# Gather indices copied by GpSimd itself, in halves of four, in a graph kernel on one Trainium2 core

## The chip, the cores and the metric

The kernel runs on one core of one Trainium2 chip. The metric is the device time of one execution in microseconds (us). Three runs of the kernel before gave 2215.43, 2211.89 and 2213.24 us, a median of 2213.24 us.

## The reference

There are 6250 nodes with 64 features each and 200000 edges, sorted by destination. Every edge takes the features of its source node, `xs = x[src]`, and five graph operators sum functions of it over the edges of each destination node:

```python
norm = edge_weights / jnp.sqrt(deg_w[src] * deg_w[dst])
gcn = seg(norm[:, None] * xs) @ Wgcn + bgcn
sage = x @ Wsage_s + seg(xs) / deg_c[:, None] @ Wsage_n + bsage
agg_w = seg(edge_weights[:, None] * xs)
gin = ((1.0 + gin_eps) * x + agg_w) @ Wgin + bgin
gconv = x @ Wgc1 + agg_w @ Wgc2 + bgc
eop = seg(edge_weights[:, None] * jax.nn.relu(xs + edge_attr)) @ Wedge + bedge
```

`seg` is the sum by destination. The five results are mixed with five weights, added to x and normalised along the features.

## The kernel before

The edges are cut into 196 chunks of 1024: 8 tiles (`TILES`) of 128 edges, one edge per partition. A chunk needs the features of its 1024 source nodes and the inverse root of their degree. Chunks get them in three ways. Chunks 0 to 15 (`EARLY`) gather raw x by an indirect DMA in the setup, before degrees are known. Chunks 16 to 35 (`PICKED`) get them by TensorE: one-hot matrices times the node table, which lies in SBUF (L1280, the picks). Chunks 36 to 195, the 160 late chunks (`LATE`), gather rows of the node table from HBM: one indirect DMA per tile, 8 per chunk, all issued by GpSimd (L559). The early chunks' remaining work is woven between the first 16 late chunks, and the picked chunks' work between the next 140 (five rounds of 28 late and 4 picked chunks). So the late chunks' loop is nearly the whole program.

A late chunk passes through the engines like this. GpSimd issues its 8 gathers into slot u of a ring of four (`feat[:, u]`, `UNROLL` = 4). VectorE (L950, L953) waits for `gathered[u]` and adds the edge attributes; ScalarE applies the ReLU (L655); VectorE weighs the one-hot matrices of the destinations (L1076); TensorE multiplies (16 matmuls of L1261) and increments `chunk_product`. GpSimd may fill the slot again only then: it waits for `chunk_product` at L556, four chunks on. Between late chunks TensorE does the picks (14 matmuls of L1280 per tile), ScalarE builds their one-hot matrices (L688, L691) and VectorE reduces them (L988, L992). Every engine works through its own list in order.

The gathers read their row numbers from `idx`, a tile at fixed addresses, [128, 4 slots, 8 tiles]. All row numbers lie in `e_src`, which a transposition in the setup fills: TensorE transposes, ScalarE copies the result out of PSUM (L590) and increments `flip_used`. ScalarE also moves row numbers from `e_src` to `idx`: for the first four late chunks once (L592), and then, at every odd slot, for the pair of slots whose gathers have landed (L650 to L653), 128x16 numbers in one copy, which increments `staged`. GpSimd waits for `staged` (L555) and for `chunk_product` (L556) ahead of each chunk. `e_src` is longer by four chunks than it need be, and L593 fills the rest, so that the last step of ScalarE's copies has something to read.

`gathers_begun` is a semaphore that nobody waits for; its increment at L557 carries the wait. In the setup GpSimd also issues the 128 gathers of the early chunks (L526): those of the first three chunks (`HEAD`) at once, the rest behind the wait for `base_stored` at L542, from the seventh chunk on paced by `weight_done` of VectorE. Then it waits for the node table in HBM (`table_stored`), and the late loop begins.

Of the kernel before, what the change touches and what calls it, by code (L numbers as in the profile page):

```python
# [27 lines left out]
U32 = mybir.dt.uint32  # L28
# [4 lines left out]
P = 128  # L33
N, D = 6250, 64
E = 200000
TILES = 8
CHUNK = P * TILES
CHUNKS = -(-E // CHUNK)
LAST_START = E - CHUNK
LAST_OLD = (CHUNKS - 1) * CHUNK - LAST_START  # L40
UNROLL = 4
# [7 lines left out]
BASE = EARLY + PICKED  # L49
LATE = CHUNKS - BASE  # L50
LATE_STEPS = LATE // UNROLL
# [20 lines left out]
HALF = TILES // 2  # L72
# [13 lines left out]
def build(nc, x, src, dst, edge_attr, edge_weight, mix, Wgcn, bgcn, Wsage_s, Wsage_n, bsage,  # L86
          gin_eps, Wgin, bgin, Wgc1, Wgc2, bgc, Wedge, bedge, out):
    ctx = ExitStack()
    with ctx:
        def sb(name, shape, dt=F32):  # L90
            return ctx.enter_context(nc.sbuf_tensor(name, shape, dt))
# [4 lines left out]
        def sem(name):  # L96
            return ctx.enter_context(nc.semaphore(name))
# [35 lines left out]
        base_row = sb("base_row", [1, CHUNKS], I32)  # L133
        passes = sb("passes", [1, 1], I32)

        e_src = sb("e_src", [P, CHUNKS + UNROLL, TILES], U32)
        e_dst = sb("e_dst", [P, CHUNKS, TILES])
        e_win = sb("e_win", [P, CHUNKS, TILES], BF16)

# [42 lines left out]
        idx = sb("idx", [P, UNROLL, TILES], U32)  # L182
# [101 lines left out]
        gathers_begun, windows_set = sem("gathers_begun"), sem("windows_set")  # L284
# [3 lines left out]
        base_ready, base_flipped, base_stored = sem("base_ready"), sem("base_flipped"), sem("base_stored")  # L288
        rows_ready, flipped, flip_used = sem("rows_ready"), sem("flipped"), sem("flip_used")
        dst_flip_used = sem("dst_flip_used")  # L290
        src_wrapped, w_lifted = sem("src_wrapped"), sem("w_lifted")
        cuts_set, sign_done, weight_done = sem("cuts_set"), sem("sign_done"), sem("weight_done")
        deg_chain, windows_moved = sem("deg_chain"), sem("windows_moved")
        deg_product, deg_added = sem("deg_product"), sem("deg_added")
# [4 lines left out]
        staged = sem("staged")  # L299
        gathered = [sem(f"gathered{u}") for u in range(UNROLL)]  # L300
# [4 lines left out]
        chunk_product = sem("chunk_product")  # L305
# [21 lines left out]
        FLIPS = 3 * 2 * (TILES // 4)  # L327
        DST_FLIPS = FLIPS // 3
# [14 lines left out]
        def node_tiles(k):  # L343

            return range(k * NODE_TILES, min((k + 1) * NODE_TILES, NT))
# [158 lines left out]
        def _(pool):  # L504
# [19 lines left out]
            def gather_early(c):  # L524
                for j in range(TILES):
                    nc.gpsimd.indirect_dma_start(  # L526
                        out=early_x[:, c, j], out_offset=None, in_=x,
                        in_offset=bass.IndirectOffsetOnAxis(ap=early_idx[:, c, j:j + 1], axis=0),
                    ).then_inc(early_gathered, 16)

            for c in range(HEAD):
                gather_early(c)
                if c == 0:
# [5 lines left out]
                    nc.gpsimd.memset(table_sb[:, :, D:TROW], 0.0).then_inc(pad_x, 1)  # L539
                    nc.gpsimd.memset(table_sb[:, N % NT:, 0:D], 0.0).then_inc(pad_x, 1)  # L540

            pool.wait_ge(base_stored, 1)  # L542
            n_pass = pool.value_load(passes[0:1, 0:1], min_val=1, max_val=WINDOWS)
            with pool.Fori(0, n_pass) as v:
                pool.wait_ge(product_g, v * UNITS + 2)
                pool.sem_inc(gathers_begun, 1)
                for c in range(HEAD, EARLY):
                    if c > PACED:
                        pool.wait_ge(weight_done, 2 * (c - PACED) - 1)
                    gather_early(c)  # L550
                pool.wait_ge(table_stored, 16)
                with pool.Fori(0, LATE_STEPS) as i:
                    for u in range(UNROLL):
                        it = v * LATE + i * UNROLL + u
                        pool.wait_ge(staged, v * (LATE // 2) + i * (UNROLL // 2) + u // 2 + 1)  # L555
                        pool.wait_ge(chunk_product, it + 1)  # L556
                        pool.sem_inc(gathers_begun, 1)  # L557
                        for j in range(TILES):
                            nc.gpsimd.indirect_dma_start(  # L559
                                out=feat[:, u, j, D:BLOCK], out_offset=None, in_=table,  # L560
                                in_offset=bass.IndirectOffsetOnAxis(ap=idx[:, u, j:j + 1], axis=0),
                            ).then_inc(gathered[u], 16)

        @block.scalar
        def _(act):
# [23 lines left out]
                        act.wait_ge(flipped, q)  # L589
                        nc.scalar.copy(flip_place(to, g, n, half), flip_of(q, n)).then_inc(flip_used, 1)  # L590
            act.wait_ge(flip_used, FLIPS - DST_FLIPS)
            nc.scalar.copy(idx[:, :, :], e_src[:, BASE:BASE + UNROLL]).then_inc(staged, UNROLL // 2)  # L592
            nc.scalar.copy(e_src[:, CHUNKS:CHUNKS + UNROLL], e_src[:, BASE:BASE + UNROLL]).then_inc(src_wrapped, 1)  # L593
            act.wait_ge(src_wrapped, 1)
            act.wait_ge(base_stored, 1)
            n_pass = act.value_load(passes[0:1, 0:1], min_val=1, max_val=WINDOWS)
            with act.Fori(0, n_pass) as v:
# [34 lines left out]
            for k in range(NODE_GROUPS):  # L632
                tiles = node_tiles(k)
# [12 lines left out]
            with act.Fori(0, n_pass) as v:  # L646
                act.wait_ge(early_gathered, early_landed(v))

                def late_chunk(i, u):
                    if u % 2:  # L650
                        act.wait_ge(gathered[u - 1], (v * LATE_STEPS + i + 1) * (16 * TILES))
                        act.wait_ge(gathered[u], (v * LATE_STEPS + i + 1) * (16 * TILES))
                        nc.scalar.copy(idx[:, u - 1:u + 1], e_src[:, bass.ds((i + 1) * UNROLL + u - 1 + BASE, 2)]).then_inc(staged, 1)  # L653
                    act.wait_ge(summed_in, v * LATE + i * UNROLL + u + 1)
                    nc.scalar.activation(feat[:, u, :, 0:D], attr[:, u], ACT.Relu).then_inc(relu_ready, 1)  # L655

# [70 lines left out]
            for g in range(GROUPS + 1):  # L727
# [5 lines left out]
                if g > 0:  # L733
                    tiles = slice((g - 1) * GROUP, g * GROUP)
# [631 lines left out]
```

## Time and profile before

| what | value |
|---|---|
| three runs | 2211.89 to 2215.43 us, median 2213.24 us |
| the profiled execution | 2228.75 us |
| its span | 2226.9 us |
| TensorE matmul (PE) busy | 1556.4 us, 70% |
| GpSimd (POOL) busy | 1355.2 us, 61% |
| VectorE (DVE) busy | 928.6 us, 42% |
| ScalarE (ACT) busy | 826.9 us, 37% |
| mean granted TensorE clock | 0.867 of full |

The span is the time from the first to the last instruction of the one profiled execution, on which all rows below rest; its own time is 2228.75 us, 15.5 us (0.7%) above the median of the three runs. Busy is the time in which an engine works on an instruction; waiting, branching and semaphores don't count. In an answer of the timeline the columns are the start, the duration, the engine, the source line, the operation, output<-input, and in brackets the idle time of the engine before the row and what ended it: "issue" means nothing that the profile shows, "remote" a semaphore whose setter the profile doesn't find close by. The ends of matmuls are modelled.

### The profile page before, as it was taken

To read this page: it belongs to the slowest core of one execution; us is meant where nothing else is said; L and a number is where in the kernel's file an instruction comes from. 1 tells how busy PE (TensorE), PEld (TensorE's weight loads), DVE (VectorE), ACT (ScalarE), POOL (GpSimd) and SP (SyncE) were. 2 spreads that over 40 slices of the span, in tenths; PEclk is the share of its full clock that TensorE was granted. 3 is DMA by queue.
4 is the path that set the end of the run, shared out by engine and by line. 5 is a ranking of instruction groups with operands and counts; after the bars stand their busy time and mean duration, and the time that the engine had idled before them with its cause. 6 is when DMAs were issued, how large, how long until landed. Compare 5 with 4: busy or idle time off the path is not lost.

```text
span 2226.9 us, 22565 instructions
## 1 busy us (share of the span) xinstructions
PE 1556.4 (70%) x6037; PEld 1007.5 (45%) x6037; DVE 928.6 (42%) x2539; ACT 826.9 (37%) x1201; POOL 1355.2 (61%) x1426
## 2 busy tenths in 40 slices
PE   1004367566888777877878778777887888877876
PEld 1003367553554544544445445444444445544546
DVE  5684256543433332433433433243333334423346
ACT  1676233243433433424244234233333324423323
POOL 7665366556666656656666666566666656665660
PEclk9999967688989888978889888888888888888988
DMA  5111234331222222222222222222222222222223
GB/s 98 23 24 51 70 100 112 95 80 42 51 64 45 55 54 46 57 46 44 54 57 53 47 57 43 47 58 50 48 66 43 48 51 57 47 53 44 59 55 77
DMA packets 83186, 126.12 MB, mean 57 GB/s; under 512 B 29494, under 2 KB 31269, under 8 KB 82821
## 3 DMA queue, kind: packets, MB, share of 16 engines
q0 software_dynamic: 45056, 48.85, 13.6%
q1 hardware_dynamic: 36371, 74.90, 11.0%
q10 hardware_dynamic: 1650, 1.04, 0.2%
q8 instruction: 53, 0.87, 0.2%
q14 instruction: 56, 0.46, 0.1%
HBM read 121.29 MB, written 3.40 MB: 56 GB/s over the span
## 4 chain that ended last, share of the span: by engine, by line
PE 43%; issue 18%; another core or an unknown queue 17%; DVE 10%; ACT 4%; POOL 3%; DVEq 2%; DMA 1%; SPq 0%; POOLq 0%; ACTq 0%
PE psum L1280 27%; PE psum L1261 13%; ACT ring L604 4%; POOL ring L559 3%; DVE ring L1076 2%; DVE sums L1065 2%; DVE early L988 1%; PE psum L1312 1%; PE psum L1228 1%; DVE attr L953 1%; DVE early L992 1%; DMA ring<-node_table,idx 1%; PE psum L1341 1%; PE psum L1342 1%
## 5 line engine op out<-in xcount | busy, mean ns | idle before, releaser
L559 POOL DMA_INDIRECT ring<-node_table,idx x1280 | 1228.4, 960 | 758.2 <-issue 389.4
L1280 PE MATMUL psum<-table_sb,early_x 128*128 128x455 f32 x2240 | 988.1, 586 | 115.6 <-issue 110.1
L1280 PEld LDWEIGHTS psum<-table_sb,early_x 128*128 128x128 f32 x2240 | 446.0, 205 | 573.4 <-issue 566.7
L1261 PE MATMUL psum<-ring 128*128 128x120 f32 x2560 | 405.3, 313 | 246.5 <-issue 127.5
L1261 PEld LDWEIGHTS psum<-ring 128*128 128x128 f32 x2560 | 375.5, 224 | 310.2 <-issue 164.9
L988 DVE TENSOR_TENSOR early<-psum,digit_hot 128x455 f32<-128x455 f32 x160 | 100.6, 631 | 989.5 <-remote 599.3
L688 ACT ACTIVATE early_x<-early,minus_ids 128x256 f32<-128x256 f16 x560 | 370.4, 744 | 138.7 <-remote 103.4
L655 ACT ACTIVATE ring<-attr 128x512 f32<-128x512 f32 x160 | 100.2, 626 | 483.4 <-DVE attr L953 383.8
L679 ACT ACTIVATE early<-early 128x256 f32<-128x256 f32 x40 | 16.7, 416 | 518.2 <-DVE early L1009 385.1
L1065 DVE TENSOR_TENSOR sums<-sums,psum 64x40 f32 (+1 forms) x648 | 127.5, 197 | 97.4 <-remote 53.6
L526 POOL DMA_INDIRECT early_x<-in_x,early_idx x128 | 122.0, 953 | 61.4 <-issue 40.3
L1261 PE MATMUL psum<-early 128*128 128x120 f32 x576 | 102.7, 340 | 77.8 <-issue 53.7
L1076 DVE TENSOR_TENSOR ring<-ring,psum 128x320 f32<-128x320 f32 x320 | 141.6, 484 | 6.0 <-issue 1.0
L691 ACT ACTIVATE early_x<-early_x,ones 128x1792 f32<-128x1792 f32 x80 | 143.1, 1788 | 2.6
L1261 PEld LDWEIGHTS psum<-early 128*128 128x128 f32 x576 | 98.0, 251 | 98.5 <-issue 72.7
L953 DVE TENSOR_TENSOR attr<-attr,ring 128x512 f32<-128x512 f32 x160 | 109.6, 685 | 0.0
L877 DVE SCALAR_TENSOR_TENSOR early<-attr,scratch,psum 128x1024 bf16<-128x1024 f32 x80 | 98.1, 1275 | 24.2 <-issue 22.6
L992 DVE TENSOR_REDUCE early<-early 128x65 f32<-128x455 f32 x160 | 98.5, 627 | 4.2
L1236 PE MATMUL psum<-ring 128*128 128x98 f32 (+1 forms) x8 | 2.0, 435 | 137.8 <-DVE ring L894 137.8
L604 ACT ACTIVATE ring<-attr,scratch 128x1024 bf16<-128x1024 f32 x82 | 93.0, 1137 | 10.6 <-issue 10.4
L1070 DVE TENSOR_TENSOR ring<-e_win,psum 128x320 f32<-128x320 f32 (+1 forms) x160 | 77.1, 482 | 18.2 <-issue 11.4
L1236 PEld LDWEIGHTS psum<-ring 128*128 128x128 f32 (+1 forms) x8 | 1.8, 327 | 138.0 <-DVE ring L894 138.0
(158 smaller groups left out, 644.8 us busy)
## 6 DMA issues: line engine op xcount, KB each, us to landing
attr<-in_edge_attr SPq DMA_DIRECT2D x79, 512.0 KB
ring<-node_table,idx POOLq DMA_INDIRECT x1280
early<-in_edge_attr SPq DMA_DIRECT2D x36, 256.0 KB
src_all<-in_src SPq DMA_DIRECT2D x16, 512.0 KB
early<-key_rows SPq DMA_DIRECT2D x10, 512.0 KB
early_x<-degree_rows SPq DMA_DIRECT2D x2, 1568.0 KB
early_x<-in_x,early_idx POOLq DMA_INDIRECT x128
node_table<-table_sb SPq DMA_DIRECT2D x1, 1666.0 KB, 6.0
```

The lines of the kernel that those rows point to most:

```text
L526: nc.gpsimd.indirect_dma_start(out=early_x[:, c, j], out_offset=None, in_=x, in_offset=bass.IndirectOffsetOnAxis(ap=early_idx[:, c, j:j + ...
L559: nc.gpsimd.indirect_dma_start(out=feat[:, u, j, D:BLOCK], out_offset=None, in_=table, in_offset=bass.IndirectOffsetOnAxis(ap=idx[:, u, j: ...
L604: last = nc.scalar.activation(signs[0:rows, k % TURNS], row_dst[0:rows, g], ACT.Sign, bias=cuts[0:rows, n:n + 1], scale=-1.0, accum_out=si ...
L688: last = nc.scalar.activation(to[:, :, a], keys[:, tile:tile + 2], ACT.Square, bias=minus_ids[:, a:a + 1])
L691: nc.scalar.activation(to, to, ACT.Relu, bias=ones[:, 0:1], scale=-2.0).then_inc(node_hot_made, 1)
L953: nc.vector.tensor_tensor(out=attr[:, u], in0=attr[:, u], in1=feat[:, u, :, D:2 * D], op=ALU.add).then_inc(summed_in, 1)
L988: nc.vector.tensor_tensor(out=picks[:, k % 2], in0=pick_ps[k % 2].rearrange("p (b c) -> p c b", b=SPLIT), in1=hot_c, op=ALU.mult).then_inc ...
L992: last = nc.vector.tensor_reduce(out=feat_g[:, half, k, D:2 * D + 1], in_=picks[:, k % 2], axis=AX.X, op=ALU.add)
L1065: last = nc.vector.tensor_tensor(out=sums[of, k, to], in0=sums[of, k, to], in1=acc[ps, part * WINDOW:(part + 1) * WINDOW], op=ALU.add)
L1076: return nc.vector.tensor_tensor(out=to[:, :, k], in0=to[:, :, 0], in1=by.unsqueeze(2).to_broadcast([P, n, WINDOW]), op=ALU.mult)
L1261: last = nc.tensor.matmul(to[:, 0:3 * WINDOW], features[:, j, 0:2 * D], hots[:, j].rearrange("p k n -> p (k n)"), start=(j == 0), stop=(j ...
L1280: last = nc.tensor.matmul(pick_ps[k % 2].rearrange("p (b c) -> p b c", b=SPLIT), node_hot[:, k, a], table_sb[:, a * SPLIT:(a + 1) * SPLIT, ...
```

## The change

GpSimd copies its row numbers itself. Ahead of the first and ahead of the fifth gather of a late chunk it copies four row numbers per partition from `e_src` to `idx`, waits for the copy's own semaphore (`staged`, now incremented by GpSimd), and goes on. Ahead of the chunk it waits for its own earlier gathers of the slot (`gathered[u]`); the wait for `chunk_product` comes behind the first copy. ScalarE's copies go (L592, L593, L653) and with them its two waits for the gathers of a pair. `e_src` loses its four extra chunks. At the start of the loops GpSimd now waits for the last transposition of `e_src` (`flip_used`), and this wait stands ahead of the early chunks 3 to 15.

```diff
-        e_src = sb("e_src", [P, CHUNKS + UNROLL, TILES], U32)
+        e_src = sb("e_src", [P, CHUNKS, TILES], U32)
...
+            pool.wait_ge(flip_used, FLIPS - DST_FLIPS)
             pool.wait_ge(base_stored, 1)
...
-                        pool.wait_ge(staged, v * (LATE // 2) + i * (UNROLL // 2) + u // 2 + 1)
-                        pool.wait_ge(chunk_product, it + 1)
-                        pool.sem_inc(gathers_begun, 1)
+                        pool.wait_ge(gathered[u], (v * LATE_STEPS + i) * (16 * TILES))
                         for j in range(TILES):
+                            if j % HALF == 0:
+                                tiles = slice(j, j + HALF)
+                                nc.gpsimd.tensor_copy(idx[:, u, tiles], e_src[:, bass.ds(i * UNROLL + u + BASE, 1), tiles].rearrange("p c j -> p (c j)")).then_inc(staged, 1)
+                                pool.wait_ge(staged, it * 2 + j // HALF + 1)
+                                if j == 0:
+                                    pool.wait_ge(chunk_product, it + 1)
+                                pool.sem_inc(gathers_begun, 1)
                             nc.gpsimd.indirect_dma_start(
...
-            nc.scalar.copy(idx[:, :, :], e_src[:, BASE:BASE + UNROLL]).then_inc(staged, UNROLL // 2)
-            nc.scalar.copy(e_src[:, CHUNKS:CHUNKS + UNROLL], e_src[:, BASE:BASE + UNROLL]).then_inc(src_wrapped, 1)
-            act.wait_ge(src_wrapped, 1)
...
                 def late_chunk(i, u):
-                    if u % 2:
-                        act.wait_ge(gathered[u - 1], (v * LATE_STEPS + i + 1) * (16 * TILES))
-                        act.wait_ge(gathered[u], (v * LATE_STEPS + i + 1) * (16 * TILES))
-                        nc.scalar.copy(idx[:, u - 1:u + 1], e_src[:, bass.ds((i + 1) * UNROLL + u - 1 + BASE, 2)]).then_inc(staged, 1)
                     act.wait_ge(summed_in, v * LATE + i * UNROLL + u + 1)
```

## Rows read from the trace of the kernel before

**Rows 1.** The page's part 5, the gathers: busy, mean ns, idle before

```profile
L559 POOL DMA_INDIRECT ring<-node_table,idx x1280 | 1228.4, 960 | 758.2 <-issue 389.4
```

**Rows 2.** Waits by engine: us in total, times, longest; the late gathers and ScalarE's ReLU

```profile
POOL ring L559 <- remote: 215.8, 69, 5.1
POOL ring L559 <- ACT idx L653: 117.4, 18, 29.2
POOL ring L559 <- PE psum L1261: 35.6, 13, 6.7
...
ACT ring L655 <- DVE attr L953: 383.8, 80, 20.1
```

**Rows 3.** Timeline of GpSimd, one run of 16 gathers and the next one's first

```profile
742.34 0.94 POOL L559 DMA_INDIRECT ring<-node_table,idx  x1 [3.85 <-remote]
...
761.05 0.94 POOL L559 DMA_INDIRECT ring<-node_table,idx  x1 [0.30 <-issue]
765.93 0.94 POOL L559 DMA_INDIRECT ring<-node_table,idx  x1 [3.94 <-remote]
```

**Rows 4.** Timelines of TensorE and VectorE in the same stretch

```profile
763.68 0.36 PE L1261 MATMUL psum<-ring 128*128 128x120 f32 x1 [1.84 <-issue]
...
765.31 0.63 DVE L988 TENSOR_TENSOR early<-psum,digit_hot 128x455 f32<-128x455 f32 x1 [10.57 <-remote]
```

**Rows 5.** Timeline of TensorE, 922 to 943 us

```profile
922.16 1.94 PE L1261 MATMUL psum<-ring 128*128 128x120 f32 x16
...
929.29 1.94 PE L1261 MATMUL psum<-ring 128*128 128x120 f32 x16
...
942.66 0.54 PE L1280 MATMUL psum<-table_sb,early_x 128*128 128x455 f32 x1 [1.61 <-issue]
```

**Rows 6.** Timeline of GpSimd beside it, 911 to 954 us

```profile
911.80 0.94 POOL L559 DMA_INDIRECT ring<-node_table,idx  x1 [2.84 <-ACT idx L653]
...
924.00 0.94 POOL L559 DMA_INDIRECT ring<-node_table,idx  x1 [2.52 <-remote]
...
953.44 0.94 POOL L559 DMA_INDIRECT ring<-node_table,idx  x1 [0.30 <-issue]
```

**Rows 7.** Timelines of GpSimd and ScalarE, end of the setup, 204 to 250 us

```profile
204.66 0.94 POOL L559 DMA_INDIRECT ring<-node_table,idx  x1 [15.90 <-issue]
...
243.35 0.94 POOL L559 DMA_INDIRECT ring<-node_table,idx  x1 [0.30 <-issue]
...
233.63 0.37 ACT L635 COPY parts_h<-psum 128x256 f32<-128x256 f32 x1 [13.47 <-remote]
...
249.75 0.37 ACT L635 COPY parts_h<-psum 128x256 f32<-128x256 f32 x1 [5.05 <-remote]
```

**Rows 8.** Timeline of GpSimd, first and last late gather behind the filled ring

```profile
273.52 1.18 POOL L559 DMA_INDIRECT ring<-node_table,idx  x1 [29.23 <-ACT idx L653]
...
2174.47 0.94 POOL L559 DMA_INDIRECT ring<-node_table,idx  x1 [0.30 <-issue]
```

**Rows 9.** Timeline of GpSimd in the setup, a small instruction behind a gather, a gather behind one

```profile
18.73 0.15 POOL L534 IOTA root_part<- 128x1 f32 x1
...
20.55 1.49 POOL L526 DMA_INDIRECT early_x<-in_x,early_idx  x1 [0.16 <-issue]
```

**Rows 10.** Timeline of ScalarE, the copy that released the gather at 273.52 us

```profile
272.38 0.19 ACT L653 COPY idx<-e_src 128x16 uint32 x1
```

**Rows 11.** Timelines of GpSimd and ScalarE in the setup, a break of about 1 us

```profile
140.73 0.94 POOL L526 DMA_INDIRECT early_x<-in_x,early_idx  x1 [1.08 <-remote]
...
143.98 1.15 ACT L604 ACTIVATE ring<-attr,scratch 128x1024 bf16<-128x1024 f32 x1 [1.21 <-issue]
```

**Rows 12.** Timelines of GpSimd and ScalarE in the setup, around the new wait

```profile
41.56 0.94 POOL L526 DMA_INDIRECT early_x<-in_x,early_idx  x1 [0.30 <-issue]
...
75.12 0.64 ACT L590 CAST e_src<-psum 128x272 uint32<-128x272 f32 x1 [10.56 <-remote]
...
187.83 0.94 POOL L526 DMA_INDIRECT early_x<-in_x,early_idx  x1 [0.30 <-issue]
```

More of the change, by code:

```diff
@@ L290, in build @@
         dst_flip_used = sem("dst_flip_used")
-        src_wrapped, w_lifted = sem("src_wrapped"), sem("w_lifted")
+        w_lifted = sem("w_lifted")
         cuts_set, sign_done, weight_done = sem("cuts_set"), sem("sign_done"), sem("weight_done")
```

## The prediction

> **What bounds the kernel now.** I read the page first: no engine is busy over 70%, and the gathers alone have 758.2 us of idle time before them [rows 1]. So I asked who waits for whom, and then read the timelines of GpSimd, TensorE and VectorE side by side.
>
> The late gathers behind the filled ring run from 273.52 to 2175.41 us [rows 8], 1901.9 us for 156 chunks, 12.19 us a chunk. Inside a run of 16 they follow each other every (761.05 - 742.34) / 15 = 1.247 us [rows 3], so a chunk costs GpSimd 9.98 us. The rest is waiting ahead of chunks: 215.8 + 117.4 + 35.6 = 368.8 us in 100 of the 160 chunk starts [rows 2]. Without the first of them (29.23 us, [rows 8]) it is 339.6 us in 99, 3.43 us each; 57 chunks start without a wait, 0.30 us behind their forerunner. GpSimd is thus the engine nearest to its limit, and what it waits for is mostly the product that frees its slot.
>
> Why is the product late? TensorE can do a late chunk and a pick in 929.29 - 922.16 = 7.13 us [rows 5]. It did so while GpSimd paused every 8 gathers (2.84 and 2.52 us, [rows 6]). Then came 24 gathers without a pause (924.00 to 954.38), and from 940 us TensorE's matmuls, which waited for no semaphore, came with holes of 1.6 us and more [rows 5]. The run of 16 shows the same: holes of 1.84 us between single matmuls until 763.68, VectorE idle for 10.57 us on a pick, and all of it over at 765.3, 3.3 us after the last gather's end at 761.99 [rows 3, 4]. At the end of the setup 32 gathers ran from 204.66 to 244.29, and a ping-pong of TensorE and ScalarE had waits of up to 13.47 us until 249.75 [rows 7]. So long unbroken runs of gathers go with an almost halted TensorE, and the halt ends some 3 to 5 us after the run. That couples the two: GpSimd runs 16 gathers, TensorE halts in the second half, GpSimd then waits 3.9 us until the halt is over.
>
> **The change, part by part.**
>
> *The copy in the middle of a chunk.* A small GpSimd instruction starts right behind a gather and takes 0.15 us [rows 9]. The gather behind it must wait for its semaphore. From below, a gather came 0.16 us after a small instruction that it didn't wait for [rows 9]; from above, one came 273.52 - 272.57 = 0.95 us after the end of the copy that released it [rows 8, 10]. A gather has 0.30 us ahead of it anyway. So a break adds between 0.01 and 0.80 us. I take 0.70, near the upper row, since the wait is of the same kind with one register step less. 156 x 0.70 = 109 us (1.6 to 125), all on GpSimd's own path; nothing covers it, and eight gathers, hence the next `gathered[u]`, land that much later. VectorE doesn't feel it as long as the ring is ahead.
>
> *The copy ahead of a chunk.* Where GpSimd waits for the product it lies under the wait. Where the product is there, the start gap becomes 0.15 + 0.95 = 1.10 us in place of 0.30. The wait for its own earlier gathers of the slot costs nothing: they landed before the product that it waits for anyway, three chunks ago.
>
> *The waits for ScalarE's copy go*: 88.2 us in 17 (117.4 less the first, [rows 2, 8]). GpSimd then waits for the product instead, which is late next: against the mean of 3.43 us the excess is 88.2 - 58.3 = 30 us.
>
> *ScalarE loses 80 copies of 0.19 us* [rows 10], 15 us of busy time, and two waits for gathers that VectorE waits for too. I cost that at nothing: ScalarE's ReLU waited 383.8 us in 80 of 160 cases for VectorE's sum [rows 2]; if that cover were gone it could give at most the 15 us.
>
> *The new wait for `flip_used`* holds the early gathers of chunk 3 on, which began at 41.56, until the last cast, at 75.76 [rows 12]. From 76.7, 13 chunks of 9.98 us end at 206.5, where they ended at 188.77 [rows 12]; the late gathers then begin 2 to 3 us later than 204.66. The 29.23 us wait ahead of chunk 4 [rows 8] hides it. But the casts themselves came in the midst of a run of gathers, the last after 10.56 us idle [rows 12], four of them 33 us apart in all. If that was the halt, the hold removes its own reason, the casts end near 48 us and ScalarE's and VectorE's long setup work starts up to 27 us earlier. Between 27 us gained and 8 lost I take 15 gained.
>
> *The sum.* Without starts a chunk's body now sums to 1901.9 - 339.6 - 57 x 0.30 = 1545.2 us. With the middle breaks 1654.4. There remain the 156 starts: to break even they may take (1901.9 - 1654.4) / 156 = 1.59 us each, where they take 2.29 now. With every product in time they take 1.10 (172 us, a gain of 76 in all). I take one start in eight with today's 3.43 us: 1.39 us each, 217 us. 1654.4 + 217 = 1871.4, a gain of 30.5 us, and 15 from the setup: 45 us. The profiled execution took 2228.75 us, 15.5 above the median; 2213.2 - 45 gives **2168 us**. This rests on one thing: that breaks of 1.1 us every four gathers, in place of 3.4 us every 8 to 16, keep TensorE from halting.
>
> **A rule against the sum.** VectorE's additions and GpSimd's work show mild contact: a gather's mean is 960 ns [rows 1] against 940 in most rows [rows 3]. The Trainium skill, SBUF — State Buffer, section Who interferes with whom, says that a VectorE instruction with two SBUF inputs contends with a GpSimd instruction that reads SBUF, for the whole instruction; the new copies read SBUF. By it a copy could be held for up to one VectorE sum; no run here shows a price yet, and the sum above doesn't contain it.
>
> **The rivals.**
>
> *Slower: breaks of 1 us are too short to end a halt* (my main rival). The place is the start of every second chunk. GpSimd's runs get longer by the breaks, and the release still comes 3 us after the run's end. Then nothing is won back: 109 us for the middles, 57 x 0.80 = 46 for the starts without a wait, less 30 for ScalarE's copies: +125, about 2335 us. For it speaks a break of 1.08 us at 140.73 in the setup, after which ScalarE still had 1.21 us holes [rows 11], and that the halts' ends follow the runs' ends so evenly [rows 3, 4, 7]. Against it speak the 10-us runs with 2.5 us breaks that left TensorE at 7.13 us a chunk [rows 5, 6]; no row shows many short breaks. It decides from a mean start of 1.59 us on. The same page of the skill (section SBUF: two separate sides) states that DMA and engine ports are disjoint, so that a DMA can't slow a compute instruction. By that rule gathers aren't the cause of the holes, breaks can't cure them, and this rival follows; rows 3 to 7 only show that they coincide.
>
> *No change:* GpSimd isn't the clock; VectorE uses the gathered rows many us after they land, and the breaks eat waits one for one: 109 us added in the middles, as much taken off the 340 us of waits; 2213 us. Against it: halts and runs are tied too closely.
>
> *Faster by more:* starts fall to 1.05, middles cost 0.65 and the setup gives its 27: 2213 - 92 - 27 = 2094 us; it is the near end of the forecast's own case.
>
> **How the numbers follow.** The forecast's case, in all its sizes from 2090 to 2208, has 0.48; no change 0.10; slower 0.42, spread from 2220 to 2380 by the bound of 0.01 to 0.80 us for a break and by how many halts remain. Under 0.2% (4.4 us) a measurement of this kernel can't tell a difference from none. The range 2090 to 2340 leaves out about 0.2, nearly all of it on the slow side. The forecast's own range is 2110 to 2205.
>
> **What would show it.** In the profile of the changed kernel: some 320 copies on GpSimd of about 0.15 us, and the gather behind each with 0.7 to 1.1 us idle; fewer and shorter waits ahead of chunks (now 3.43 us); TensorE's late products 8 to 11 us apart without holes; waits on ScalarE's `idx` gone; the last cast of `e_src` at about 48 us rather than 75.8. I am wrong if the holes in TensorE's picks remain, if the waits ahead of chunks stay near 3.4 us, or if a break costs well over 1 us since its own semaphore comes late too.

## The result and the profile after

Four runs of the kernel before have a median of 2212.56 us (2209.07 to 2215.43), four of the changed kernel 2122.24 us (2120.59 to 2124.56). The ratio is 0.9593, with a 95% interval of 0.9576 to 0.961: 90.3 us faster, where 45 had been forecast. The two profiled executions differ by more, 104.1 us, since that of before was 16 us above its median and that of after 2 us. The ledger below is kept in spans; 14 of its 104 us belong to that one execution.

The page of the changed kernel, parts 1, 4 and 5:

```profile
span 2122.8 us, 23385 instructions
PE 1527.1 (72%) x6037; PEld 1018.6 (48%) x6037; DVE 937.5 (44%) x2539; ACT 824.9 (39%) x1119; POOL 1422.0 (67%) x1746
...
POOL 42%; issue 36%; PE 8%; ACT 6%; DVE 3%; another core or an unknown queue 2%; POOLq 2%; DMA 1%; DVEq 0%; SPq 0%; ACTq 0%
...
L565 POOL DMA_INDIRECT ring<-node_table,idx x1280 | 1230.9, 962 | 579.9 <-issue 496.7
L1279 PE MATMUL psum<-table_sb,early_x 128*128 128x455 f32 x2240 | 926.9, 566 | 4.7 <-issue 3.2
```

The idle time ahead of the gathers is 579.9 us [rows 1 had 758.2]. The picks are the second row to read: 2240 matmuls with 4.7 us of idle time ahead of them. Such idle time, which no wait explains, is called holes below. On the page of before the same group (L1280) read:

```profile
L1280 PE MATMUL psum<-table_sb,early_x 128*128 128x455 f32 x2240 | 988.1, 586 | 115.6 <-issue 110.1
```

The holes in the picks are nearly gone. Their matmuls also became shorter, 566 ns in place of 586, at a mean granted clock of 0.891 in place of 0.867; e5 below has 564 ns at 0.894 and no holes on another chip, so a clock of this height doesn't make the holes. GpSimd's waits, changed kernel (total us, times, longest):

```profile
POOL ring L565 <- POOL idx L560: 74.3, 91, 0.9
...
POOL ring L565 <- remote: 6.3, 5, 1.7
POOL ring L565 <- PE psum L1260: 2.6, 3, 0.9
```

A wait for a product occurs 8 times at most [rows 2 had 100 waits of 368.8 us, 18 of them for ScalarE's copy]; what stands there now is GpSimd's wait for its own copy. Its timeline, one chunk:

```profile
703.58 0.20 POOL L560 COPY idx<-e_src 128x4 uint32 x1
704.65 0.96 POOL L565 DMA_INDIRECT ring<-node_table,idx  x1 [0.87 <-issue]
705.92 0.94 POOL L565 DMA_INDIRECT ring<-node_table,idx  x1 [0.30 <-issue]
...
709.37 0.19 POOL L560 COPY idx<-e_src 128x4 uint32 x1
710.35 0.96 POOL L565 DMA_INDIRECT ring<-node_table,idx  x1 [0.79 <-POOL idx L560]
...
715.07 0.19 POOL L560 COPY idx<-e_src 128x4 uint32 x1
```

Gather to gather across a break, the gap is 704.65 - 703.58 = 1.07 us ahead of a chunk and 710.35 - 709.36 = 0.99 us in its middle, in nearly all of the 156 chunks. Where the loop begins and ends:

```profile
204.74 0.18 POOL L560 COPY idx<-e_src 128x4 uint32 x1 [12.79 <-DMA node_table<-table_sb]
205.83 0.96 POOL L565 DMA_INDIRECT ring<-node_table,idx  x1 [0.91 <-POOL idx L560]
...
252.82 0.96 POOL L565 DMA_INDIRECT ring<-node_table,idx  x1 [0.88 <-issue]
...
2080.15 0.94 POOL L565 DMA_INDIRECT ring<-node_table,idx  x1 [0.31 <-issue]
```

Against [rows 8] (273.52 to 2175.41, in a span of 2226.9) the span's difference has three parts. **Ahead of chunk 4** 20.7 us. **The loop** 1901.9 - 1828.3 = 73.6 us: all gaps ahead of chunks, summed over the trace, fell from 357.3 to 168.3 us, the gaps in the middle rose from 47.5 to 155.3, those ahead of a chunk's second gather from 61.1 to 67.5, and the gathers took 1.3 us more. **Behind the last gather** 51.5 - 41.7 = 9.8 us.

### The profile page after: what moved, and what is told of

It is laid out like the page before. It is cut to its first block, busy times and chain, and to the rows that moved or that the text cites. A ratio compares the mean times of both kernels' runs of the same rounds, so it can differ in the third digit from the quotient of the medians.

```text
span 2122.8 us, 23385 instructions
## 1 busy us (share of the span) xinstructions
PE 1527.1 (72%) x6037; PEld 1018.6 (48%) x6037; DVE 937.5 (44%) x2539; ACT 824.9 (39%) x1119; POOL 1422.0 (67%) x1746
## 4 chain that ended last, share of the span: by engine, by line
POOL 42%; issue 36%; PE 8%; ACT 6%; DVE 3%; another core or an unknown queue 2%; POOLq 2%; DMA 1%; DVEq 0%; SPq 0%; ACTq 0%
POOL ring L565 39%; ACT ring L607 4%; PE psum L1260 3%; POOL idx L560 3%; PE psum L1279 1%; PE psum L1227 1%; PE psum L1311 1%; POOLq L560 1%; ACT early L660 1%; PE psum L1340 1%; PE psum L1341 1%; PE psum L1222 0%; DMA sums<-in_dst 0%; DMA ring<-node_table,idx 0%
## 5 line engine op out<-in xcount | busy, mean ns | idle before, releaser
L565 POOL DMA_INDIRECT ring<-node_table,idx x1280 | 1230.9, 962 | 579.9 <-issue 496.7
L1279 PE MATMUL psum<-table_sb,early_x 128*128 128x455 f32 x2240 | 926.9, 566 | 4.7 <-issue 3.2
L1260 PE MATMUL psum<-ring 128*128 128x120 f32 x2560 | 432.7, 335 | 329.9 <-ACT ring L654 168.2
L1279 PEld LDWEIGHTS psum<-table_sb,early_x 128*128 128x128 f32 x2240 | 435.0, 200 | 414.4 <-issue 412.7
L1260 PEld LDWEIGHTS psum<-ring 128*128 128x128 f32 x2560 | 399.9, 243 | 405.7 <-issue 223.9
L949 DVE TENSOR_TENSOR psum<-e_w,ring 128x8 f32<-128x8 f32 x160 | 28.6, 178 | 673.7 <-DMA ring<-node_table,idx 673.7
L952 DVE TENSOR_TENSOR attr<-attr,ring 128x512 f32<-128x512 f32 x160 | 109.9, 687 | 0.0
```

The source lines that it names most:

```text
L565: nc.gpsimd.indirect_dma_start(out=feat[:, u, j, D:BLOCK], out_offset=None, in_=table, in_offset=bass.IndirectOffsetOnAxis(ap=idx[:, u, j: ...
L952: nc.vector.tensor_tensor(out=attr[:, u], in0=attr[:, u], in1=feat[:, u, :, D:2 * D], op=ALU.add).then_inc(summed_in, 1)
L1260: last = nc.tensor.matmul(to[:, 0:3 * WINDOW], features[:, j, 0:2 * D], hots[:, j].rearrange("p k n -> p (k n)"), start=(j == 0), stop=(j ...
L1279: last = nc.tensor.matmul(pick_ps[k % 2].rearrange("p (b c) -> p b c", b=SPLIT), node_hot[:, k, a], table_sb[:, a * SPLIT:(a + 1) * SPLIT, ...
```

## The experiments

The late loop has 40 steps of four chunks, 32 gathers; times of a step are differences of the starts of first gathers. Nothing but what is said was changed, and the row numbers gathered are the same.

**The four first experiments**, with each one's edit.

e1, a break in the middle of the chunk, ScalarE's copies kept:

```diff
                         for j in range(TILES):
+                            if j == HALF:
+                                nc.gpsimd.tensor_copy(spare[:, :], idx[:, u, HALF:TILES]).then_inc(paused, 1)
+                                pool.wait_ge(paused, it + 1)
+                                pool.sem_inc(gathers_begun, 1)
```

> The kernel before, with ScalarE's index copies and its order as they are, plus one break in the middle of each late chunk: GpSimd copies 4 numbers to a spare tile, waits for the copy's own semaphore and goes on to the fifth gather. Theory (unbroken runs of gathers of over some 10 us halt TensorE; any break of about 1 us prevents it): the holes in the picks go, the run is as fast as the changed kernel or faster, since a start with everything ready costs 0.30 us and not 1.09: middles 156 x 0.69 = 108 us, starts near 0.3 to 1.1 us, 2010 to 2110 us. Rival (the gain comes from taking the copy, and with it the wait for landed gathers, from ScalarE): the waits stay and the break is added, 2213 + 60 to 108 = 2270 to 2320 us.

e2, the half split undone in the changed kernel:

```diff
-                            if j % HALF == 0:
+                            if j == 0:
...
-                                nc.gpsimd.tensor_copy(idx[:, u, tiles], e_src[:, bass.ds(i * UNROLL + u + BASE, 1), tiles]...
+                                nc.gpsimd.tensor_copy(idx[:, u, :], e_src[:, bass.ds(i * UNROLL + u + BASE, 1)]...
```

> The changed kernel with the half split undone: GpSimd copies all 8 numbers in one go ahead of the chunk, so a run is 8 gathers (9.7 us) and not 4 (4.7 us). Theory that runs up to some 10 us leave TensorE alone: 156 middle breaks of 0.69 us go, 2122 - 108 = 2014 us, up to 2060 if TensorE's order becomes the limit here and there. Rival (a break of 1.1 us every 8 gathers is too rare; the half split is what cures the halts): holes in the picks return, waits ahead of chunks of 2 us and more, 2130 to 2210 us.

e3, one copy of 16 numbers ahead of every second chunk in the changed kernel:

```diff
+                                if u % 2 == 0:
+                                    nc.gpsimd.tensor_copy(idx[:, u:u + 2, :], e_src[:, bass.ds(i * UNROLL + u + BASE, 2)]).then_inc(staged, 1)
```

> The changed kernel with one copy of 16 numbers ahead of every second chunk: GpSimd still copies its own indices and ScalarE none, but runs are of 16 gathers (19.7 us) unless a product is late. Theory (the length of the run decides): the holes in the picks come back in the second half of each run, waits of 3 to 4 us ahead of every second chunk, 2130 to 2213 us. Rival (GpSimd copying for itself is the gain, breaks are only a cost): the fastest of all, about 2122 - 108 - 78 x 0.79 = 1952 us, at most 2014 us.

e4, the kernel before with the new wait for `flip_used` alone (the hold):

```diff
+            pool.wait_ge(flip_used, FLIPS - DST_FLIPS)
             pool.wait_ge(base_stored, 1)
```

> The kernel before with nothing but the wait for flip_used ahead of the early gathers 3 to 15. Theory (the hold gives the casts a stretch without gathers): the last cast of e_src moves from 75.8 to about 45 us, the gain up to the loop is 0 to 20 us, 2192 to 2213 us. Rival (the 21 us that the changed kernel won ahead of chunk 4 come from the breaks in the 32 gathers that fill the ring, not from the hold): no change, 2209 to 2217 us, though the casts are early.

Measured: the kernel before itself took **1829.69 us** on this chip (13 runs, 1827.71 to 1832.19), not 2212.56. e1 took 1941.74 us (1.0613, interval 1.0596 to 1.0631), e2 1970.43 (1.0776, 1.0759 to 1.0794), e3 1915.01 (1.0467, 1.045 to 1.0485), e4 1830.72 (1.0003, 0.9993 to 1.0013). No theory had this in it. On this chip there is no halt to cure, so these four runs say nothing of the cure and only give the price of breaks: e1's middles cost 156 x 0.69 = 108 us by the sum, and e1 is 112 us slower. Nor is GpSimd's copying a gain in itself here: e3, with the fewest breaks, loses 85 us.

**e5 and e6: both kernels again**, to learn whether this is a state of a chip or of a run. Neither has an edit.

> The changed kernel itself, beside the kernel before on the same chip. On the chip of the first four experiments the kernel before takes 1829.7 us, not 2212.6: no wait ahead of any late chunk but the 0.30 us, no holes in the picks. Theory A (the halts are a state of the chip or core that a job lands on, and the change only helps where they occur): if the kernel before again takes about 1830 us, every break is a pure loss, 156 x (0.69 + 0.79) = 231 us and some 5 to 10 for the four chunks that fill the ring, 2060 to 2075 us, slower by 12 to 13%; if it takes about 2213 us, the changed kernel takes 2118 to 2126 us again. Theory B (the changed kernel repairs something and reaches the 1830 us level elsewhere too): 1830 us or less.

> The kernel before itself, for its trace on this chip. Theory A: either the first chip's picture (late stretch 1902 us, 340 us of waits ahead of chunks, holes in the picks) and 2213 us, or the other's (late stretch of 156 x 8 gathers at 1.25 us = 1560 to 1570 us, no waits, no holes) and 1830 us, with nothing between. Theory B (the state varies from run to run on any chip): a time between them, or one off the median of the runs beside it by over 1%.

Measured, on yet another chip: before 1830.27 us (7 runs, 1826.44 to 1831.34), changed kernel 2092.91 us, ratio **1.1445 (1.1426 to 1.1464)**. Theory A (the halts belong to a chip or its state) held, and the time is 18 us above its range. The change that wins 4% on one chip loses 14% on another. Page of the kernel before on this chip:

```profile
span 1831.0 us, 22565 instructions
PE 1426.6 (78%) x6037; PEld 941.1 (51%) x6037; DVE 933.7 (51%) x2539; ACT 835.5 (46%) x1201; POOL 1348.9 (74%) x1426
...
L559 POOL DMA_INDIRECT ring<-node_table,idx x1280 | 1221.7, 954 | 390.0 <-issue 389.1
L1280 PE MATMUL psum<-table_sb,early_x 128*128 128x455 f32 x2240 | 899.0, 553 | 0.0
```

GpSimd's waits in the same execution:

```profile
POOL ring L559 <- issue: 389.1, 1277, 0.3
...
POOL ring L559 <- PE psum L1261: 0.9, 3, 0.3
```

No late gather waits longer than 0.3 us, and the picks have 0.0 us of idle time: 1568.8 us for 156 chunks, 1.257 us a gather. GpSimd is the limit, and every break is on it. Summed over the loops of e5 and e6, gaps ahead of chunks grew by 118.3 us, middles by 106.9, gaps ahead of second gathers by 20.0, the gathers by 4.3: together 249.5, as much as the loop grew (1818.2 - 1568.8 = 249.4). The 20.0 us are the part that theory A lacked. I call chips where the kernel before takes 1830 us free, and those where it takes some 2200 us halting.

**e7 and e8: several patterns of breaks in one kernel.** ScalarE's copies stay; GpSimd's loop is cut into stretches, and the breaks are waited copies to a spare tile, so that one trace compares patterns on one chip (`STRETCHES` and `PAUSES` stand for the list and the number that the kernels have written out; the copy that nobody waits for is left out here):

```diff
-                with pool.Fori(0, LATE_STEPS) as i:
+                for first, last, waited, loose, base, per in STRETCHES:
+                    with pool.Fori(first, last) as i:
...
+                                for _ in range(waited.get((u, j), 0)):
+                                    nc.gpsimd.tensor_copy(spare[:, :], e_src[:, 0, 0:HALF]).then_inc(paused, 1)
+                                    pool.wait_ge(paused, v * PAUSES + (i - first) * per + base + n)
+                                    pool.sem_inc(gathers_begun, 1)
```

> The kernel before (ScalarE's copies kept), with GpSimd's late loop cut into five stretches: steps 0 to 11 as before; 12 to 18 a small copy ahead of the fifth gather that nobody waits for; 19 to 25 the same copy with a wait for its semaphore (runs of 8); 26 to 32 such a waited copy ahead of every second chunk only (runs of 16); 33 to 39 ahead of the first and the fifth gather, as in the changed kernel (runs of 4). A step is 4 chunks. Cost of a break where nothing halts: step 39.9 us as before; 40.0 to 41; 39.9 + 4 x 0.69 = 42.7; 39.9 + 2 x 0.79 = 41.5; 39.9 + 4 x (0.69 + 0.79) = 45.8 us, and the kernel takes 1830 + 28 x 0.69 + 14 x 0.79 + 28 x 1.48 = 1902 us. Where the kernel before takes 2213 us (chip with halts), theory (run length decides): 48.8; 48.8 if the copy must be waited for, 40 to 43 if any GpSimd instruction will do; 42.7 to 44; 46 to 50; 45.8. Rival (only breaks of every 4 gathers cure it): the third stretch also at 46 to 50 us.

> The kernel before (ScalarE's copies kept); in steps 0 to 4 a waited copy ahead of the fifth gather of each chunk, then five stretches of 7 steps in which k = 1, 2, 3, 4, 5 such copies one behind the other stand ahead of every second chunk, so runs stay at 16 gathers and the break grows by about 0.8 us each time. Where nothing halts: steps of 39.9 + 2 x 0.8 k = 41.5, 43.1, 44.7, 46.3, 47.9 us and 1830 + 20 x 0.69 + 14 x 0.8 x 15 = 2012 us. Where the kernel before takes 2213 us: the halts sit in the second half of each run of 16, whatever the break, so the steps don't sink below 45 us, and the wait for the product shrinks as the break grows (theory: run length); rival (break length): above some k the holes are gone and the step equals the sum without halts.

Measured, on a third chip: before 2212.89 us, so the picture of the first measurement was found again; e7 2193.26, e8 2217.88 us. First gathers of e7's steps 5, 12, 19, 26 and 33, and its last:

```profile
488.71 0.95 POOL L573 DMA_INDIRECT ring<-node_table,idx  x1 [19.27 <-PE psum L1275]
...
819.99 0.95 POOL L573 DMA_INDIRECT ring<-node_table,idx  x1 [3.90 <-remote]
...
1155.09 0.95 POOL L573 DMA_INDIRECT ring<-node_table,idx  x1 [5.15 <-ACT idx L667]
...
1487.86 0.97 POOL L573 DMA_INDIRECT ring<-node_table,idx  x1 [0.80 <-POOL spare L570]
...
1822.23 0.97 POOL L573 DMA_INDIRECT ring<-node_table,idx  x1 [0.80 <-POOL spare L570]
...
2147.92 0.95 POOL L573 DMA_INDIRECT ring<-node_table,idx  x1 [0.30 <-issue]
```

Between two of these rows lie seven steps, so a step is a seventh of the difference (the last row is taken to its end and 0.30 us on). A step takes 47.3 us without breaks, 47.9 with a copy that nobody waits for, 47.5 with a waited one per chunk (42.7 expected, and 46 to 50 by the rival), 47.8 with one per two chunks, 46.7 with two per chunk. How much a stretch scatters is seen in e11 below, one pattern on the same chip: its five stretches take 47.1, 47.7, 47.7, 47.9 and 48.0 us, with 21.3 to 39.2 us of holes in the picks. So of e7's five only the last stands out, by its time barely and by its holes clearly: 0.8 us, where the other four have 13.7 to 18.9:

```profile
L1294 PE MATMUL psum<-table_sb,early_x 128*128 128x455 f32 x439 | 180.9, 564 | 0.8 <-issue 0.7
```

Runs of 8 with one short break aren't enough: my expectation for e2, 2014 us, was wrong for a halting chip too. And since ScalarE's copies stay in e7, the last stretch settles a rival: the breaks alone bring a step to the changed kernel's 46.7 us, whoever copies the row numbers. In e8 the break stood behind the wait for the product and each further copy added 0.35 us, not 0.8; the steps took 47.7, 47.8, 48.4, 48.2 and 49.3 us, and 19.9 us of holes remained at five copies, though the gap ahead of a run of 16, the wait for the product and the copies together, was then mostly 5 us. Whether a break that stays long once the product is there would cure runs of 16 stays open: the longest tried is 2.4 us.

**e9 to e11: length of the run or rate.** e9 takes the form of e7 with other breaks (its list, put in words; steps 0 to 4 and 12 to 18 have runs of 4), e10 is the kernel e2, e11 the kernel e4.

```diff
+                for first, last, waited, loose, base, per in STRETCHES:
...
+  steps 5 to 11:  {(0,0): 1, (0,5): 1, (1,2): 1, (2,0): 1, (2,5): 1, (3,2): 1}
+  steps 19 to 25: {(u,0): 2}
+  steps 26 to 32: {(u,0): 3}
+  steps 33 to 39: {(u,0): 1, (u,2): 1, (u,4): 1, (u,6): 1}
```

> The kernel before (ScalarE's copies kept) with six stretches of breaks made of waited GpSimd copies: steps 0 to 4 and 12 to 18 runs of 4; 5 to 11 runs of 5, 5 and 6; 19 to 25 runs of 8 with a break of two copies; 26 to 32 runs of 8 with three copies; 33 to 39 runs of 2. Where nothing halts a step is the sum: 39.9 + 4 x (0.69 + 0.79) = 45.8; 39.9 + 6 x 0.72 = 44.2; 45.8; 39.9 + 4 x 1.6 = 46.3; 39.9 + 4 x 2.4 = 49.5; 39.9 + 16 x 0.7 = 51.1 us. Where the kernel before takes 2213 us, theory A (length of the unbroken run, a limit between 5 and 8 gathers): 44 to 45 in the second stretch, holes in the fourth and fifth as with any runs of 8. Theory B (a rate: halts come when GpSimd issues more than one gather per some 1.45 us over several runs, whatever the split): the second stretch holes again and at 46.5 to 48 us, the fourth about 46.3 to 47 with few holes, the fifth and sixth at their sums without holes.

> The half split undone again (GpSimd copies all 8 numbers ahead of the chunk, runs of 8, breaks of 1.02 us), now hoped for on a chip with halts. If the kernel before takes 2213 us there, theory B (rate; runs of 8 give one gather per 1.34 us): holes return, a late step of 47 to 48.5 us, 2150 to 2200 us, so the half split made the gain. Theory A (run length with a limit above 8): 2122 - 108 = 2014 us. If the kernel before takes 1830 us there: 1970 us, as in the first run of this kernel.

> The kernel before with only the wait for flip_used ahead of the early gathers 3 to 15. If the kernel before takes 2213 us there: the last cast of e_src moves from 75.8 to about 45 us, and the time falls by 0 to 15 us, since the late gathers still begin at 204 to 206 us and the halt of the 32 filling gathers (69 us for step 0, 47 in the changed kernel) stays: theory, most of the 21 us won ahead of chunk 4 is from the breaks. Rival (the hold gives them): 2185 to 2195 us. If it takes 1830 us: no change again.

Measured: the chip of e7 and e8 again, before 2201.95 us (12 runs, a wide 2185.79 to 2226.6). e9 2172.07 us. First gathers of its steps 1, 5, 12, 19, 26, 33, and the last gather:

```profile
251.82 1.11 POOL L573 DMA_INDIRECT ring<-node_table,idx  x1 [0.79 <-issue]
...
442.50 0.97 POOL L573 DMA_INDIRECT ring<-node_table,idx  x1 [0.80 <-issue]
...
771.67 0.97 POOL L573 DMA_INDIRECT ring<-node_table,idx  x1 [0.79 <-POOL spare L570]
...
1100.21 0.96 POOL L573 DMA_INDIRECT ring<-node_table,idx  x1 [0.79 <-POOL spare L570]
...
1434.12 0.97 POOL L573 DMA_INDIRECT ring<-node_table,idx  x1 [0.79 <-issue]
...
1762.45 0.97 POOL L573 DMA_INDIRECT ring<-node_table,idx  x1 [0.79 <-POOL spare L570]
...
2126.51 0.94 POOL L573 DMA_INDIRECT ring<-node_table,idx  x1 [0.30 <-issue]
```

The groups of lines give TensorE's holes in the picks for the five stretches from step 5 on (busy us, mean ns, idle before):

```profile
L1294 PE MATMUL psum<-table_sb,early_x 128*128 128x455 f32 x455 | 195.5, 577 | 7.6 <-issue 6.8
...
L1294 PE MATMUL psum<-table_sb,early_x 128*128 128x455 f32 x471 | 198.8, 574 | 1.9 <-issue 1.4 <-DVE early L1002 0.5
...
L1294 PE MATMUL psum<-table_sb,early_x 128*128 128x455 f32 x426 | 192.3, 593 | 18.5 <-issue 18.2
...
L1294 PE MATMUL psum<-table_sb,early_x 128*128 128x455 f32 x451 | 197.2, 587 | 7.4 <-issue 4.8 <-DVE early L1002 2.3
...
L1294 PE MATMUL psum<-table_sb,early_x 128*128 128x455 f32 x433 | 178.3, 564 | 0.0
```

With the measured price of each break (0.69 us for one copy, 0.35 for each more) and 39.9 us for 32 gathers, the sums stand against the measured steps as below. Two things that no break explains come on top and are measured in each stretch, together 0.7 to 1.3 us a step: a late second gather (below) and gathers that take longer than 0.94 us. What is left then is in the column "rest", and is for the most part waits for products:

| breaks | sum, us | measured, us | rest, us | holes in the picks, us |
|---|---|---|---|---|
| runs of 5, 5, 6 | 44.0 | 47.0 | 1.9 | 7.6 |
| runs of 4 | 45.4 | 46.9 | 0.3 | 1.9 |
| runs of 8, two copies | 44.1 | 47.7 | 2.9 | 18.5 |
| runs of 8, three copies | 45.5 | 46.9 | 0.5 | 7.4 |
| runs of 2 | 50.9 | 52.2 | 0.0 | 0.0 |

Theory A (a limit on the run between 5 and 8) asked for 44 to 45 us in the first line and got 47.0 with holes: refuted. Theory B (a limit on the rate) has the first line right. In the third it asked for 46.3 to 47 us with few holes, and got 47.7 with the most of all; in the fourth it asked for the sum without holes and got holes, but there the break is shorter than I had reckoned (45.5 us and not 49.5). So a rate by itself isn't shown either. For it speaks that the lines with sums of 45.4 us and more run within 0.5 us of what is asked, those with 44.0 and 44.1 don't, and no stretch of seven steps on a halting chip took less than 46.5 us (e12's, below), 1.45 us a gather, where a free chip does 1.257. Against it speak e8 and the kernel before. With five copies e8's sum is 39.9 + 2 x 2.09 = 44.1 us, as in the first and third line, but the step is 49.3: at one sum, runs of 5 to 6, 8 and 16 take 47.0, 47.7 and 49.3 us. And at 1.54 us a gather in that stretch, and at 1.51 in the kernel before, holes are there all the same. What the runs show is thus narrower: on halting chips runs of 4 and of 2 with breaks of 0.69 us leave 0.0 to 2.3 us of holes in a stretch of seven steps (the changed kernel, e7, e9), and every pattern with longer runs 3.2 to 39.2 (the kernel before, e7 to e11). Both the length of a run and the distance between gathers seem to count, by what rule stays open; a limit on the length of 4 gathers fits all but the short rest of the fourth line.

e10 took 2165.08 us (ratio 0.984, 0.9762 to 0.9919), in theory B's range; 2122 - 108 = 2014 is refuted. Its waits, GpSimd:

```profile
POOL ring L563 <- remote: 156.2, 59, 3.9
...
POOL ring L563 <- PE psum L1258: 40.3, 7, 21.8
```

So 196.5 us of waits for products came back in 66 cases with the half split undone, 8.9 in the changed kernel. Its late steps take 46.9 us, its five stretches 46.7 to 47.1 with 3.2 to 25.0 us of holes. e11 took 2209.96 us (1.005, 1.0015 to 1.0084): the hold alone gives nothing, if anything a loss of half a per cent, and the rival (2185 to 2195 us) is refuted. In its trace, ScalarE's last cast and GpSimd's first gathers of chunks 0 and 4:

```profile
44.82 0.65 ACT L591 CAST e_src<-psum 128x272 uint32<-128x272 f32 x1 [0.32 <-PE psum L1212]
...
205.92 0.94 POOL L560 DMA_INDIRECT ring<-node_table,idx  x1 [13.62 <-issue]
...
273.98 1.18 POOL L560 DMA_INDIRECT ring<-node_table,idx  x1 [28.41 <-ACT idx L654]
```

The cast is 30 us earlier than in [rows 12], the loop begins when it did, and chunk 4 waits as in [rows 8]. In e9, with runs of 4 and no hold, chunk 4 begins at 251.82. The 21 us of the setup thus come from breaks in the 32 gathers that fill the ring.

**e12: breaks in the early gathers too**, since the loop starts at 206 us on a halting chip and at 178 on a free one:

```diff
-                    gather_early(c)
+                    gather_early(c, v)
...
+                    if v is not None and j % HALF == 0:
+                        nc.gpsimd.tensor_copy(spare[:, :], early_idx[:, c, 0:HALF]).then_inc(paused, 1)
+                        pool.wait_ge(paused, v * (2 * (EARLY - HEAD)) + 2 * (c - HEAD) + j // HALF + 1)
+                        pool.sem_inc(gathers_begun, 1)
```

> The changed kernel with the same kind of break (a waited copy to a spare tile) also ahead of the first and fifth gather of each early chunk from the fourth on: 26 breaks of 0.69 us in the setup. Where the kernel before takes 2200 to 2213 us: on chips without halts the late gathers begin at 178 us, here at 206, as the early gathers run unbroken; with the breaks the halts of the setup go, the late gathers begin at 180 to 196 us and the time is 2122 less 10 to 20 us, 2100 to 2112 us. Rival (the pacing of the early gathers costs what the halts gave): 2118 to 2130 us. Where the kernel before takes 1830 us: 2093 us as the changed kernel, up to 18 us more.

Measured, on another halting chip: 2114.02 us (six runs, 2111.79 to 2116.6) beside 2208.22 for before, ratio 0.9566 (0.9535 to 0.9597). The late gathers begin at 200.36 us, where 180 to 196 had been expected. The median is 8 us below the changed kernel's 2122.24, between what the theory (2100 to 2112) and the rival (2118 to 2130) asked for, and the two intervals of the ratio overlap; that it is the faster of the two is likely and not shown. On a free chip nothing that ran was faster than the kernel before.

## Why the prediction was right and wrong

On a chip like the one that the rows came from, direction and mechanism held: breaks of 1 us every four gathers keep TensorE from halting, and GpSimd then goes by its own sum. On a free chip the same forecast would have had the wrong sign; nothing in the rows told the two apart. The time lay in the range (2090 to 2340) and in the forecast's own range; the gain was twice the one forecast. Term by term, in spans:

- *The break in the middle*: 0.70 us forecast, 0.99 - 0.30 = 0.69 measured, 108 us in all. Right.
- *A start with everything ready*: 1.10 forecast, 1.07 measured. Right.
- *The mean start* is the step that failed. I took "one start in eight with today's 3.43 us", 1.39 us each and 217 us in all. Measured: 168.3 us in 155 starts, 1.09 each; 3 waits for the product by name and 5 by a remote semaphore, none above 1.7 us. The sum had the floor in it (a gain of 76 us in the loop with every product in time, where 73.6 came) and no row spoke for the eighth. It was a hedge put into a term, where it belonged in the range. This is 43 of the missing us, net of 6 for the second gathers.
- *The setup*: 15 us forecast, 20.7 measured, but for a wrong reason. The casts did end early (45.0 us, forecast 48), which earned nothing (e4, e11); the breaks in the filling of the ring did, which I had not costed, though [rows 7] show that stretch as the longest run of all.
- *The tail*: 0 forecast, 9.8 measured. Behind the last gather the changed kernel takes 41.7 us, as before does on a free chip (1831.0 - 1789.4 = 41.6). So the halt of the last run was in the 51.5 us. The other halting runs bear it out: those whose last gathers come in runs of 2 or 4 (e7, e9, e12) have 41.5 to 42.7 us there, those with longer runs (e8, e10, e11) 46.7 to 51.5.
- *The profiled executions*: that of before lay 16 us above its median, that of after 2 us, so 14 of the 104 us between the spans are not in the medians. Together 45 + 43 + 6 + 10 - 14 = 90.

By parts of the edit, on halting chips: the hold 0 (e11), the copies of GpSimd with one break per chunk 35 us (e10: 1.6% of 2202, compared on one chip; the interval allows 18 to 52), the split in halves 2165 - 2122 = 43 us (compared across chips). They make 78 and not 90, as the kernel before took 11 us less on e10's chip than in the first measurement. Of the 43, 2158.6 - 2122.8 = 36 us are in the spans, and only 14 of them in the loop: 17 lie ahead of chunk 4, where e10 still waits 21.8 us for a product, and 5 behind the last gather.

The main rival (breaks of 1 us too short) fell for four gathers a run. But it describes e10 and e7's runs of 8 well: there the waits go on. That the 10-us runs of [rows 5, 6] left TensorE alone was a reading of one pattern with 2.5 us breaks; runs of 8 with breaks of 1 us halt, and so do e9's runs of 5 and 6. The changed kernel, at (2081.1 - 447.0) / 35 = 46.7 us a step, takes 0.2 us more than on a free chip (46.5 in e5): next to nothing is left of the halts there. "GpSimd isn't the clock" is refuted on free chips by e6 and in the changed kernel's first profile by the chain, which is now 42% POOL and 36% issue against 43% PE before.

The rule that compute engines and DMAs don't meet in SBUF (the Trainium skill, SBUF — State Buffer, section SBUF: two separate sides) led to a rival here. On free chips the traces agree with it: 0.0 us of holes in the picks beside unbroken gathers. On halting chips holes vanish when the gathers come in runs of 4 or 2 and return when they don't, in one trace (e9); there the measurement decides that something that goes with the gathers holds TensorE. Whether it is their issue on GpSimd or their transfers, and whether the engines then lack data or instructions, no run shows. The rule on VectorE against a GpSimd instruction (the Trainium skill, same page, section Who interferes with whom) bears on the copies:

```profile
L560 POOL COPY idx<-e_src x320: 183/192/727, 204.7 to 2075.0; 128x4 uint32 x160
```

Minimum, median and longest are 183, 192 and 727 ns. The timelines of VectorE and GpSimd show what the long ones met, a sum (L952, both inputs in SBUF) and, for the longest, a comparison (L968):

```profile
422.40 0.68 DVE L952 TENSOR_TENSOR attr<-attr,ring 128x512 f32<-128x512 f32 x1
422.59 0.54 POOL L560 COPY idx<-e_src 128x4 uint32 x1
...
390.74 0.69 DVE L968 TENSOR_SCALAR early<-early 128x1024 f32<-128x1024 f32 x1
390.74 0.73 POOL L560 COPY idx<-e_src 128x4 uint32 x1
```

The copy of 422.59 ends at 423.13, the sum at 423.08. The same holds for all three copies that began under an L952 sum, for one under L1102 and for seven under L1008, which are such sums too: each ended 0.04 to 0.05 us behind the sum or had its usual length, whichever was later. That agrees with the rule. The longest copy ends 0.04 us behind L968, which reads a single tile; the rule as cited doesn't speak of such an instruction. With 64.3 us for 320 copies against 320 x 0.192 = 61.4 all such meetings cost 3 us.

What stays open: what differs between the chips, whether it is the chip or a state that it is in for a time, and which resource limits halting ones. Late landing of the gathers isn't it: in the profiled execution of before, the last of a gather's packets starts 2.1 to 2.2 us after the gather's start in the median, at the first place of a run as at the sixteenth.

## What to carry to other kernels

A kernel tuned around a stall should be measured on several chips first: the same pair read 0.9593 and 1.1445, each within fractions of a per cent from run to run. Where engines with no wait show holes while GpSimd issues gathers, try shorter runs of gathers, and price the breaks (here 0.69 us each) against the waits they take away: only runs of 4 and less left no holes to speak of here. A trace of one pattern scatters by about 1 us a step from stretch to stretch, so compare holes as well as times. And when a sum has a floor that the mechanism reaches, forecast the floor or name the row that keeps it away.

## What was not expected of the hardware

- Two kinds of chips: 2202 to 2213 us for the same program on halting ones (the first measurement, then two chips), 1830 on free ones (two chips). Neither kind changed within a set of runs; only one chip, a halting one, was met again in a later set (e7 and e8, then e9 to e11).
- On halting chips no stretch of seven steps got below 1.45 us a gather, whatever the pattern, though each gather takes 0.94 us on GpSimd and lands on time.
- In the loops with GpSimd's own copies the second gather of a step's third chunk is late by 1.5 us in 13 of 39 steps, with no wait to explain it, on both kinds of chips. In the kernel before this is absent on a free chip (e6) and present in 9 of 39 steps on a halting one. A row of the changed kernel:

```profile
517.25 0.97 POOL L565 DMA_INDIRECT ring<-node_table,idx  x1 [0.87 <-issue]
520.05 0.94 POOL L565 DMA_INDIRECT ring<-node_table,idx  x1 [1.83 <-issue]
```
